# Sparsifying of the feed-forward part in three pieces between chunks; Silu and tile copies ahead of the rotation's parts

## The reference

```python
q = _rope((x @ w_q.T)...); k = _rope((x @ w_k.T)...); v = (x @ w_v.T)...
...
def _rope(x): ... return x * cos + rot * sin
...
def _sparsify_2to4(h):
    g = h.reshape(B, S, I // 4, 4)
    _, idx = jax.lax.top_k(jnp.abs(g), 2)
    mask = (pos == idx[..., 0:1]) | (pos == idx[..., 1:2])
    return (g * mask).reshape(B, S, I)
h = jax.nn.silu(x @ w_gate) * (x @ w_up)          # I = 1024
y = _sparsify_2to4(h) @ w_down
```

## Time and profile before

| | us |
|---|---|
| time, median of 3 runs (2078.84 to 2084.3) | 2079.32 |
| the profiled execution: its own time | 2079.05 |
| its span, first to last instruction | 2077.1 |
| PE busy (10042 instructions) | 1750.2 (84%) |
| VectorE busy (2366) | 1191.6 (57%) |
| ScalarE busy (1316) | 805.7 (39%) |
| GpSimd busy (252) | 254.5 (12%) |

### The profile page before, as it was taken

The page is one execution under the profiler, slowest core; times in us unless marked ns, Lnnn a source line. Parts: engine busy times, 40 slices in busy tenths (PEclk is TensorE's granted clock), DMA queues, the critical chain, the costliest instruction groups (busy, mean ns, idle before and its releaser), DMA issues.

```text
span 2077.1 us, 27028 instructions
## 1 busy us (share of the span) xinstructions
PE 1750.2 (84%) x10042; PEld 1091.0 (53%) x10043; DVE 1191.6 (57%) x2366; ACT 805.7 (39%) x1316; POOL 254.5 (12%) x252
## 2 busy tenths in 40 slices
PE   4999999869778996569988989987989888989897
PEld 3788888745447995323344443343533344433345
DVE  5556666451562005577755668656767666667455
ACT  4444444212230100227654227743146633157520
POOL 4334333212240000100010000000000000000000
PEclk8999999889995556758899989898988999979999
DMA  2000000040012420200000000000000000000000
GB/s 93 14 28 21 30 20 20 11 137 25 10 31 84 125 87 0 84 0 2 1 1 0 1 1 1 22 0 0 1 1 1 21 0 0 1 1 2 21 0 21
DMA packets 27139, 47.83 MB, mean 23 GB/s; under 512 B 7312, under 2 KB 16016, under 8 KB 26256
## 3 DMA queue, kind: packets, MB, share of 16 engines
q1 hardware_dynamic: 26464, 44.74, 6.6%
q0 software_dynamic: 576, 1.77, 0.3%
HBM read 37.59 MB, written 9.06 MB: 22 GB/s over the span
## 4 chain that ended last, share of the span: by engine, by line
issue 58%; POOL 2%; DVE 0%; POOLq 0%; DVEq 0%
POOL rs_sb L1251 1%; POOL ve_sb L1248 0%; POOL qks_sb L1266 0%; POOL v_sb L1265 0%; POOL qks_sb L1256 0%; DVE bn_sb L1431 0%; DVE x_sb_sb L1446 0%; POOLq L1086 0%; POOLq L65 0%; POOL qks_sb L1267 0%; DVE mv_sb L1437 0%; DVEq L1086 0%; POOL v_sb L1264 0%; DVEq L65 0%; DVEq L1435 0%
## 5 line engine op out<-in xcount | busy, mean ns | idle before, releaser
L1488 DVE TENSOR_REDUCE mx_sb<-s_ps 128x1 f32<-128x512 f32 (+1 forms) x512 | 322.7, 655 | 137.1 <-PE s_ps L1742 93.0
L1319 ACT ACTIVATE room_sb<-s_ps 128x1024 f32<-128x1024 f32 (+1 forms) x320 | 282.5, 949 | 22.7 <-PE s_ps L1766 20.0
L1739 PE MATMUL s_ps<-room_sb 48*128 48x512 f16 (+3 forms) x640 | 206.6, 355 | 18.0 <-DVE mx_sb L1483 9.6
L1766 PE MATMUL s_ps<-room_sb 51*128 51x128 f16 (+4 forms) x1152 | 155.4, 297 | 34.7 <-ACT room_sb L1319 26.5
L1786 PE MATMUL cm_ps<-room_sb,v_sb 128*32 128x512 f32 (+3 forms) x1536 | 179.3, 550 | 0.8 <-ACT room_sb L1325 0.8
L1739 PEld LDWEIGHTS s_ps<-room_sb 48*128 48x128 f16 x640 | 60.2, 99 | 225.9 <-DVE mx_sb L1488 134.3
L1248 POOL TENSOR_TENSOR ve_sb<-mv_sb,eps_sb 128x4 f32<-128x4 f32 x24 | 5.0, 210 | 1195.1 <-DVE mv_sb L1437 1195.1
L1898 PE MATMUL s_ps<-xbT_sb,w_fg_sb 128*128 128x512 f32 x256 | 132.6, 630 | 13.8 <-DVE room_sb L1534 13.0
L1911 PE MATMUL cm_ps<-w_fd_sb,room_sb 128*128 128x256 f32 x512 | 131.0, 405 | 14.2 <-DVE room_sb L1562 14.2
L1898 PE MATMUL s_ps<-xbT_sb,w_fu_sb 128*128 128x512 f32 x256 | 130.2, 620 | 0.0
L392 DVE SCALAR_TENSOR_TENSOR x_sb_sb<-xp_sb,conv_w_sb,x_sb_sb 128x512 f32<-128x512 f32 x96 | 108.5, 1139 | 22.8 <-ACT x_sb_sb L319 20.5
(11 more groups left out here) (233 smaller groups left out, 3513.3 us busy)
## 6 DMA issues: line engine op xcount, KB each, us to landing
we_gu_sb<-we_gu SPq DMA_DIRECT2D x32, 352.0 KB
we_dn_sb<-we_dn SPq DMA_DIRECT2D x32, 176.0 KB
x_in_sb<-x SPq DMA_DIRECT2D x9, 512.0 KB, 3.7
rows<-x_sb_sb SPq DMA_DIRECT2D x8, 512.0 KB, 3.0
x_sb_sb<-rows SPq DMA_DIRECT2D x2, 2048.0 KB, 12.3
out<-x_sb_sb SPq DMA_DIRECT2D x8, 512.0 KB, 2.6
xp_sb<-w_in SPq DMA_DIRECT2D x1, 1024.0 KB, 5.6
x_sb_sb<-w_up SPq DMA_DIRECT2D x1, 1024.0 KB, 6.4
```

What stands on the lines that cost most here:

```text
L1319: act.activation(weights[(g * NU + u) % SLOTS_P][:, 2 * pair:2 * pair + 2, 0:width(u) * P], W[s % 2][:, :, 0:width(u) * P], ACT.Exp, scale ...
L1488: dve.tensor_reduce(mx[:, pair, k % 2, slot:slot + 1], X[:, k % 2, 0:count * P], AX.X, ALU.max, negate=True).then_inc(mx_ok, 1)
L1739: last = pe.matmul(X[:, k % 2, at * P:(at + plain) * P], query[head:head + NORM, i * P:(i + 1) * P], key[head:head + NORM, j * P:(j + plai ...
L1766: last = pe.matmul(W[s % 2][:, head, (at + low - i) * P:(at + high - i) * P], key[first:first + rows, j * P:(j + 1) * P], query[first:firs ...
```

## The change

The block of `sparsify` is cut into `compare` (L1549 to L1551 of before), `count` (L1553 to L1560) and `keep_largest` (L1562). For block k they run after the hidden products of steps 4k + 4, 4k + 5 and 4k + 6, one in each, where before all three ran after that of step 4k + 3. `hj` gets a second buffer, so that the next block can be written meanwhile (the buffer `ctok` of the attention, which is not read in this stage). In the stages with a next sequence `compare` and `count` of block 1 both stand behind step 8 and `keep_largest` behind step 9; blocks 2 and 3 are sparsified in one as before. In the last stage blocks 0 to 2 are cut. On ScalarE `xt_copied` and `silu` now stand ahead of `high_part`, and the magnitude of step 4 moves behind that of step 5. TensorE's list, the transfers and GpSimd's list are the same. The number of VectorE and ScalarE operations is the same.

```diff
@@ magnitude (ScalarE)
-                wait(act, hs_ok, 4 * b + w // 4)
-                act.activation(aj[:, w % 4, :], hj[:, w % 4, :], ACT.Abs).then_inc(ab_ok, 1)
+                if w >= 4 or b > 0:
+                    wait(act, sp, 3 * (4 * b + w // 4 - 1) + 1)
+                act.activation(aj[:, w % 4, :], hj[w // 4 % 2][:, w % 4, :], ACT.Abs).then_inc(ab_ok, 1)
@@ steps of ScalarE
                 for w in range(16):
-                    if ahead and w + 1 < ST:
-                        high_part(c, w + 1)
                     if ahead and w + 2 < ST:
                         xt_copied(c, w + 2)
                     if w == HALF_AT:
                         second_chunk(b, 1)
                     silu(b, w)
                     if ahead and w + 1 < ST:
+                        high_part(c, w + 1)
                         part_copies(c, w + 1)
                     if ahead and w in (NF, NF + 1):
                         qk_copied(c, 0, w - NF, 1)
                         qk_copied(c, 0, w - NF, 0)
-                        if w > NF:
+                    if w not in (4, NF):
+                        if w in (5, NF + 1):
                             magnitude(b, w - 1)
-                            magnitude(b, w)
-                    else:
                         magnitude(b, w)
@@ hidden (VectorE)
                 if w % 4 == 0:
-                    wait(dve, hs_ok, 4 * b + w // 4)
-                    wait(dve, ab_ok, 16 * b + w)
+                    wait(dve, hs_ok, 4 * b + w // 4 - 1)
+                    wait(dve, ab_ok, 16 * b + w - 4)
@@ sparsify is cut into these
+            def compare(b, k):
+                wait(dve, ab_ok, 16 * b + 4 * k + 4)
+                wait(dve, hs_ok, 4 * b + k)
...
+            def count(b, k):
...
+            def keep_largest(b, k):
+                wait(dve, sp, 3 * (4 * b + k) + 3)
                 if k == 0:
                     wait(dve, fd_mm, 4 * b)
                 if k == 3:
                     wait(dve, fd_mm, 4 * b + 2)
...
+            def sparsify(b, k):
+                compare(b, k)
+                count(b, k)
+                keep_largest(b, k)
@@ steps of VectorE
-                    if w % 4 == 3:
-                        sparsify(b, w // 4)
+                    if w >= 4 and w % 4 == 0:
+                        compare(b, w // 4 - 1)
+                    if w >= 4 and w % 4 == 1 or ahead and w == NF:
+                        count(b, w // 4 - 1)
+                    if w >= 4 and w % 4 == 2:
+                        keep_largest(b, w // 4 - 1)
                     if not ahead and w == DOWN_AT:
                         residual(b, 0)
+                if not ahead:
+                    sparsify(b, 3)
                 if ahead:
                     for w in range(10, 12):
                         m = 4 * (w - 10)
                         maxima(c, 0, m, m + 2)
                         hidden(b, w - 1)
+                        if w == 10:
+                            keep_largest(b, 1)
                         maxima(c, 0, m + 2, m + 4)
```

More of the change, by code:

```diff
@@ L1067, in width @@
     return sum(count for _, _, count in UNITS[unit][1])
[L1070 to L1082, removed]
 def attention_ffn_phase(nc, io, keep):
@@ L1130, in attention_ffn_phase @@
         hs = carve(3 * 4 * 512).rearrange("p (k c) -> p k c", k=12)
-        hj = carve(4 * 512).rearrange("p (k c) -> p k c", k=4)
+        hj = [a.rearrange("p (k c) -> p k c", k=4) for a in
+              (carve(4 * 512), ctok[:, :, :].rearrange("p t c -> p (t c)"))]
         aj = carve(4 * 512).rearrange("p (k c) -> p k c", k=4)
@@ L1531, in hidden, with row @@
                 if w % 4 == 0:
-                    wait(dve, hs_ok, 4 * b + w // 4)
-                    wait(dve, ab_ok, 16 * b + w)
[L1534 to L1539, removed]
+                    wait(dve, hs_ok, 4 * b + w // 4 - 1)
+                    wait(dve, ab_ok, 16 * b + w - 4)
+                dve.tensor_tensor(hj[w // 4 % 2][:, w % 4, :], S[w % ring(b)][:, 1, :], sgl[:, w % 2, :], ALU.mult).then_inc(hm_ok, 1)
+            def compare(b, k):
+                own = aj
+                wait(dve, ab_ok, 16 * b + 4 * k + 4)
+                wait(dve, hs_ok, 4 * b + k)
+                def row(i, m):
+                    return own[:, i:i + 1, :].to_broadcast([P, m, 512])
+                dve.tensor_tensor(ge[:, 0:3, :], row(0, 3), own[:, 1:4, :], ALU.is_ge)
+                dve.tensor_tensor(ge[:, 3:5, :], row(1, 2), own[:, 2:4, :], ALU.is_ge)
+                dve.tensor_tensor(ge[:, 5, :], own[:, 2, :], own[:, 3, :], ALU.is_ge).then_inc(sp, 1)
+            def count(b, k):
+                s = 3 * (4 * b + k)
+                wait(dve, sp, s + 1)
+                dve.tensor_tensor(nb[:, 0, :], ge[:, 0, :], ge[:, 1, :], ALU.add)
+                dve.tensor_tensor(nb[:, 1, :], ge[:, 3, :], ge[:, 4, :], ALU.add)
+                dve.tensor_tensor(nb[:, 2, :], ge[:, 1, :], ge[:, 3, :], ALU.add)
+                dve.tensor_tensor(nb[:, 3, :], ge[:, 2, :], ge[:, 4, :], ALU.add).then_inc(sp, 1)
+                wait(dve, sp, s + 2)
+                dve.tensor_tensor(nb[:, 0, :], nb[:, 0, :], ge[:, 2, :], ALU.add)
+                dve.tensor_tensor(nb[:, 1, :], nb[:, 1, :], ge[:, 0, :], ALU.subtract)
+                dve.tensor_tensor(nb[:, 2, :], nb[:, 2, :], ge[:, 5, :], ALU.subtract)
+                dve.tensor_tensor(nb[:, 3, :], nb[:, 3, :], ge[:, 5, :], ALU.add).then_inc(sp, 1)
+            def keep_largest(b, k):
+                wait(dve, sp, 3 * (4 * b + k) + 3)
                 if k == 0:
@@ L1543, in sparsify @@
                     wait(dve, fd_mm, 4 * b + 2)
[L1544 to L1550, removed]
[L1551 to L1560 removed]
                 for i, (op, bound) in enumerate(((ALU.is_ge, 2.0), (ALU.is_ge, 1.0), (ALU.is_le, 0.0), (ALU.is_le, 1.0))):
[L1562 removed]
+                    last = dve.scalar_tensor_tensor(hs[:, k % 3 * 4 + i, :], nb[:, i, :], bound, hj[k % 2][:, i, :],
+                                                    op, ALU.mult)
                 last.then_inc(hs_ok, 1)
[L1564 removed]
+            def sparsify(b, k):
+                compare(b, k)
+                count(b, k)
+                keep_largest(b, k)
             def attn_residual(b, s):
```

11 lines of the change are left out of this document (removed).

## The result

The changed kernel takes 2007.6 us (median of 5 runs, 2005.71 to 2009.24) against 2079.32 (2075.28 to 2084.3, 5 runs): ratio 0.9655, 95% interval 0.9638 to 0.9671. The profiled execution took 2007.36.

The account below looks back on a forecast made before the run. PE was taken as the bound, losing time where it stands still or gets its lower clock. Stages of 16.6, 14.9 and 18.0 (49.5) plus 4.2 in the last make 53.7, from 2079.05 to 2025 us; range 2015 to 2045.

Parts of the forecast that it names:

- C: Step 10: g(10) waits 3.14 us for hidden product 8 behind block 1's sparsify; 1.6 given back, net 1.5.
- Waits, 12.56 us a stage: A stage: 3.55 at A, 1.1 in steps 1 to 3, 7.77 at B, 3.14 at C, less new waits 1.4, 1.6.
- I take half, 1.1: Steps 1 to 3: half of 2.17 us of transposes and small tile-copy waits goes (bounds 0 and 2.2).
- A: Step 0: PE waits 3.55 us for copied tile 2, behind the high part; clock adds 1.35; new wait 1.4.
- B: Step 4: PE idles 7.77 us, the rotation being behind a whole sparsify; clock adds 2.70, together 10.5 saved.
- Clock in the stages, 11.8 us in all: Low clock gone behind A (1.35), B (2.70), none at C; stages 1, 2 differing by -1.73 and +1.35 us.
- The clock in the attentions between, which I take as unchanged: In the attentions between the stages: the clock stays as it was; no size given.
- B hidden, slack 0.8: Steps 5 to 8: VectorE's pieces stay hidden; hidden 6 done at 12.7, g(8) due 13.5; hidden 7 at 16.5, g(9) 16.9.
- Rival 1: VectorE is late in steps 5 to 8, giving 2038.5 or 2049.5 us; chance 0.13.
- rival 3: The loop through Silu becomes the bound, each of seven steps growing by 3.53 us: 2095, slower; chance 0.04.
- The last stage, 4.2: Last stage: waits of 1.55 (g(7)) and 2.05 (g(11)) and 1.6 of low clock go; 1.0 given back at the end.
- rival 2: The clock falls at the new waits, two in each of three stages, one in the last: 18.9 back, 2044; chance 0.05.

Follow-up runs that it names:

- e9: Kernel before with TensorE's long idle stretches in the first three stages filled by matmuls that serve nothing; 2056.6 us, ratio 0.988.
- e4: Kernel before with eight additional matmuls in TensorE's idle time at B, ahead of the projection of tile 6; 2072.98 us, ratio 0.9964.
- e6: Changed kernel with ScalarE's q, k, v copies ahead of the magnitude and, in the last stage, block 2's count and keep_largest right behind its comparisons; 2010.93 us.
- e12: Changed kernel with e6's moves and block 3 in two halves of 256 tokens in the last stage alone; 2003.6 us, ratio 0.9648.
- e11: Changed kernel unaltered, run a third time; 2006.75 us, ratio 0.9643.
- e8: Changed kernel with three additional matmuls in the idle time before the last down projection of the first three stages; 2005.91 us, ratio 0.9663.
- e10: e6's kernel with idle time before the last down projection filled, three matmuls in each of the first three stages, four in the last; 2003.12 us.
- e15: Changed kernel unaltered, a single execution for a fourth profile; 2004.46 us.
- e5: Kernel before, unaltered, a single execution for a second profile; 2085.69 us.

## Why the prediction was wrong

The direction, the places and what would come in their stead were right; the sum, 53.7, fell short of the 73.1 that the means of four profiles each give (60.3 in the stages, 8.2 in the attentions, 5.0 in the last stage, -0.4 ahead of all). The steps that failed are the clock in the attentions, taken as unchanged (8.2 us), the waits of a stage (7.5 us in three) and the clock in the stages (3.3 us), above all behind C. The time lies 7.4 us below the range, and the first step alone is more than that. By its own steps:

1. *Waits, 12.56 us a stage (3.55 + 1.1 + 7.77 + 3.14 - 1.4 - 1.6).* They were worth 15.1 (e9 against the changed kernel, both at full clock), 7.5 more in three stages. Start to start in the first stages of both traces the six terms are 3.81, 2.14, 8.04, 3.31, -1.14 and -1.09, which makes 15.07. The largest error is "I take half, 1.1" for steps 1 to 3: steps 1, 2 and 5 each lost 0.6 to 0.9 to a tile copy behind the high part, 2.14 together. In e9's trace:

```profile
1089.33 1.98 PE L1699 MATMUL s_ps<-w_qk_sb,xt_sb 128*128 128x512 f32 x4 [0.62 <-ACT xt_sb L1282]
1096.19 1.98 PE L1699 MATMUL s_ps<-w_qk_sb,xt_sb 128*128 128x512 f32 x4 [0.36 <-ACT xt_sb L1282]
1124.44 1.98 PE L1699 MATMUL s_ps<-w_qk_sb,xt_sb 128*128 128x512 f32 x4 [0.36 <-ACT xt_sb L1282]
```

In the trace of before, stage 1 has the same three waits (0.61, 0.36, 0.36); stage 0, from which the term was taken, ran at the low clock just ahead of the first and the third of them and shows only part. The new waits were priced above what they were, A 1.14 for 1.4, C 1.09 for 1.6. And the idle time of a row is short: a row of four such matmuls is 1.88 long while the next starts 1.72 after it, so each of A, B and C is about 0.17 longer than its row says, and behind A and B the first row reaches the next after 1.82 us instead of 1.72. At B, in e9's trace, the projection begins 7.94 us after the last matmul of u(4) gave way to the filling ones (1109.64 to 1117.58), against the 7.77 of the earlier trace rows.

2. *Clock in the stages, 11.8 us in all.* It was 15.1 (60.3 less 45.2). The step that failed is "in the 3 us of idling at C it stayed 1.00", taken from stage 0 for all. The stretch behind g(10) of stage 1 in the same trace has it low behind C:

```profile
1445.00:1449.00 4.00, 4.00 (x9) 0.61 0.00 0
1449.00:1453.00 4.00, 4.00 (x8) 0.54 0.00 0
```

In the four profiles of before the clock fell behind C in 7 of 12 stages, 1.5 to 3.1 us each, 4.3 us in three stages on the mean, where the sum has nothing. Behind A, stage 0's 1.35 is no rule either: projection to g(1) takes 2.69 us in stage 1 and 5.28 in stage 2, against 3.93. The stretches of rows 1 end at g(10), ahead of it, so carrying stage 0's terms over by their difference lost it again.

3. *"The clock in the attentions between, which I take as unchanged".* It moved, by 8.2 us, with the same instructions and no less idle time: the largest single miss. The prediction puts this term at nothing and gives no reason for it. It was named as what would make the prediction wrong, but has no part in the range either.

4. *B hidden, slack 0.8.* Right: no wait at g(8) or g(9) in any of the four profiles of the changed kernel. Hidden products 6 and 7 in the changed kernel's first stage:

```profile
1118.18 0.68 DVE L1519 TENSOR_TENSOR ctok_sb<-s_ps,sgl_sb 128x512 f32<-128x512 f32 x1
1122.04 0.69 DVE L1519 TENSOR_TENSOR ctok_sb<-s_ps,sgl_sb 128x512 f32<-128x512 f32 x1
```

They end 1.2 us ahead of g(8) (1120.08) and 1.7 us ahead of g(9) (1124.41), a little more than the 0.8 and 0.4 that were worked out. Rival 1 (VectorE late) and rival 3 (the loop through Silu) didn't happen; new waits came only where forecast.

5. *The last stage, 4.2.* 5.0, with the two waits at its end as described.

6. *The rule on the clock* (the Trainium skill, TensorE: Matmul & The Clock Gate, Part 1: the throttled state is the default, and activity releases it). The new waits of 0.95, 0.71 and 0.29 us brought no low clock: it is 1.00 throughout in 10 of the 12 stages of the four profiles, and in the other two it had fallen 0.2 us ahead of the stage. Of the old waits in the four profiles of before, B's 7.8 us brought it in all 12 stages, A's 3.6 in 9 and C's 3.1 in 7; and e4 (at B) and e9 show that giving PE something to do in them keeps it away. The trace agrees with the rule in that; the strict reading that the prediction gave it, rival 2, does not hold for waits under 1 us.

How much is what, then, of the 73: some 45 us are waits in the first three stages, 15 the clock in them, 5 the last stage, 8 the clock in the attentions. **Open** remains what sets the clock in an attention: the means of before and of the changed kernel lie 8.2 apart where four executions of one kernel range over 7.4 and 6.4. It doesn't go by how much the stage ahead idles (e6 and e12 against the changed kernel), and stages alike to 0.01 us are followed by attentions that differ by 2.4 (e11: 148.96, 150.73, 148.30). The idle stretch at the attention's start is one cause of low clock, as e8's first ten matmuls show; what filling it is worth in all differs between e8 (no gain in the median) and e10 (some 7 us against e6). In e6 and e12 stages shorter by 0.5 us go along with attentions 6 us longer, a profile each; that the alignment of small gaps does it is a guess that no run here isolates.

## What to carry to other kernels

Price a removed stall with its clock, and look at every repetition of it: here the same wait at C cost 3.1, 4.7 or 6.2 us depending on the stage, and one repetition tells nothing about the next. A stretch that is to stand for a stage must end behind the last thing that the change touches. In an engine's list, what waits for a slow partner belongs behind what others wait for; a long block that nobody needs soon is best cut so that each piece fits into the slack of one step. If the clock fluctuates, 2 us that are clearly won in one stretch can be gone in the sum, so small mends need their stretch compared, not only the total.

## What was not expected of the hardware

With the clock at 1.00 a stage repeats to 0.01 us (128.11, 128.11, 128.12), while an attention, whose PE waits are all 1.9 us or shorter past its start, takes from 145.7 to 157.0 us with the same instructions, at a mean granted clock from 0.95 down to 0.85. The shortest of the eight profiles' (e15, the second) and the longest (e5, the second), PE alone:

```profile
1463.38:1609.03 145.65, 124.33 (x1141) 0.95 0.02 8
1506.01:1662.96 156.95, 136.36 (x1141) 0.85 0.02 8
```

Filling idle time on TensorE with matmuls that serve nothing made the kernel before 1.2% faster (e9, 0.96% to 1.44%).
